# A transformer layer with test-time training: the two MLP weights are read transposed from memory

## The reference, cut to what matters

```python
x = x + layernorm(attn(layernorm(x)))
x = x + layernorm(ffn(layernorm(x)))

def attn(x):                      # 4 heads of 64 for the learned part, 2 of 128 for the attention
    qkv = x @ Wqkv
    q, k, v = heads(silu(qkv))    # q and k divided by their norms
    # scan over 4 chunks of 128 rows, with fast weights W0, W1, W2 and momenta M0, M1, M2 per head
    #   out  = (silu(q W0') * (q W2')) W1'
    #   dW   = gradient of the same form on k, v, times learned rates, plus momentum
    #   W    = renorm(W + newtonschulz5(dW))           # 5 iterations
    ttt = rms_norm(out) * o_norm_g * silu(x @ Ws + bs)
    att = sliding_window_softmax(q_, k_, v_)           # window 128, 2 heads
    return (ttt + att) @ Wo

def ffn(x):
    h = gelu(x @ proj1.T + proj1_bias)                 # proj1 is 1024 x 256
    return h @ proj2.T + proj2_bias                    # proj2 is 256 x 1024
```

## Time and profile before

| | |
|---|---|
| median of 3 runs | 418.66 us (416.7 to 420.85) |
| the profiled execution | 421.38 us, span 419.6 us |
| PE busy | 387.9 us (92%) |
| PE weight loads busy | 311.2 us (74%) |
| DVE busy | 274.4 us (65%) |
| ACT busy | 225.7 us (54%) |
| POOL busy | 195.6 us (47%) |
| mean granted clock of PE | 0.995 of full speed |

### The profile page before, as it was taken

How to read it: one execution, slowest core, us unless ns; L and a number is a source line. 1 busy time by engine, 2 the same in 40 slices (tenths; PEclk the granted TensorE clock), 3 DMA queues, 4 the chain that set the end, 5 groups by cost and what they waited for, 6 DMA issues and landing times.

```text
span 419.6 us, 15701 instructions
## 1 busy us (share of the span) xinstructions
PE 387.9 (92%) x6574; PEld 311.2 (74%) x6574; DVE 274.4 (65%) x720; ACT 225.7 (54%) x444; POOL 195.6 (47%) x273
## 2 busy tenths in 40 slices
PE   5989997999999999999998999988989899997994
PEld 5578766886678869788667888587788647885883
DVE  3468998787265879997446874986667763576013
ACT  1699556466942178646985452654446674433510
POOL 4386671658532524784240874263234260366014
PEclk9999999999999999999999999999999999998999
DMA  5811000000000000030000000001200000020001
GB/s 155 297 39 52 2 2 4 5 4 3 2 4 2 14 2 2 26 118 5 3 2 5 3 2 0 2 2 55 54 5 3 5 1 2 0 74 28 2 0 51
DMA packets 12293, 10.83 MB, mean 26 GB/s; under 512 B 4160, under 2 KB 11712, under 8 KB 12224
## 3 DMA queue, kind: packets, MB, share of 16 engines
q1 hardware_dynamic: 12224, 9.83, 7.5%
HBM read 7.73 MB, written 2.10 MB: 23 GB/s over the span
## 4 chain that ended last, share of the span: by engine, by line
PE 63%; DVE 9%; issue 6%; POOL 5%; DMA 1%; ACT 1%; POOLq 0%; DVEq 0%; SPq 0%; ACTq 0%
PE pair L780 14%; PE pair L789 9%; PE pair L682 6%; PE pair L670 5%; PE pair L695 5%; PE pair L659 4%; PE pair L748 3%; PE pair L564 3%; POOL fro L1386 2%; PE pair L715 2%; PE pair L536 2%; PE pair L621 1%; PE pair L607 1%; POOL u_n L1386 1%; DMA x<-in_L_attn_x_dram 1%
## 5 line engine op out<-in xcount | busy, mean ns | idle before, releaser
L780 PE MATMUL pair<-xn2T,p1T 128*128 128x512 f32 (+1 forms) x160 | 59.8, 524 | 0.6 <-ACT xn2T L813 0.6
L789 PE MATMUL pair<-p2T,h 128*128 128x256 f32 x256 | 56.7, 380 | 0.0
L1391 POOL TENSOR_SCALAR var<-mv 128x1 f32<-128x1 f32 (+1 forms) x52 | 12.4, 238 | 91.8 <-DVE mv L1355 58.8
L789 PEld LDWEIGHTS pair<-p2T,h 128*128 128x128 f32 x256 | 48.2, 190 | 6.5
L780 PEld LDWEIGHTS pair<-xn2T,p1T 128*128 128x128 f32 x160 | 30.5, 197 | 20.0 <-issue 17.5
L1057 DVE SCALAR_TENSOR_TENSOR A<-pair,eye 128x512 f32<-128x512 f32 x45 | 28.6, 684 | 14.3 <-PE pair L670 14.2
L820 ACT ACT_TABLE_LOAD x28 | 35.9, 1283 | 2.1 <-PEq L1532 1.7
L1057 DVE SCALAR_TENSOR_TENSOR B<-pair,eye 128x512 f32<-128x512 f32 x45 | 28.9, 683 | 11.7 <-PE pair L682 11.7
L1033 ACT ACTIVATE h<-pair,b 128x512 f32<-128x512 f32 (+1 forms) x40 | 23.6, 602 | 21.9 <-PE pair L780 21.7
L1386 POOL TENSOR_TENSOR rstd<-var,neg_half 128x1 f32<-128x1 f32 (+1 forms) x52 | 31.7, 610 | 4.3
L682 PE MATMUL pair<-A 64*64 64x64 f32 x1440 | 28.7, 222 | 5.4 <-issue 5.4
(11 more groups left out here) (166 smaller groups left out, 837.2 us busy)
## 6 DMA issues: line engine op xcount, KB each, us to landing
x_in<-in_L_attn_x_dram SPq DMA_DIRECT2D x4, 512.0 KB, 4.3
h<-in_L_ffn_proj_dram SPq DMA_DIRECT2D x2, 1024.0 KB, 6.7
x<-in_L_attn_x_dram SPq DMA_DIRECT2D x4, 512.0 KB, 4.5
out_dram<-rows_a SPq DMA_DIRECT2D x16, 128.0 KB, 1.7
wqkv<-in_L_attn_Wqkv_dram SPq DMA_DIRECT2D x1, 768.0 KB, 5.5
wo<-in_L_attn_Wo_dram SPq DMA_DIRECT2D x1, 256.0 KB, 7.8
X<-in_L_attn_w_dram SPq DMA_DIRECT2D x6, 32.0 KB, 2.4
b<-in_L_ffn_proj_bias_dram SPq DMA_DIRECT2D x1, 128.0 KB, 4.3
```

Source lines behind the costliest of these rows:

```text
L780: mm_ = pe.matmul(ps[:, at], p1T[:, k, n * P:(n + 1) * P], xn2T[:, k, at], start=(k == 0), stop=(k == KC - 1))
L789: mm_ = pe.matmul(ps[:, 0:DIM], h[:, n, b * P:(b + 1) * P], p2T[:, n, :], start=(n == 0), stop=(n == HC - 1))
```

## The change

The host lays proj1 and proj2 out transposed, as 256 x 1024 and 1024 x 256 arrays, before the launch. SP loads them straight into `p1T` and `p2T`. The eight `MT` steps are gone from `ORDER`, from PE and from ACT, with the two views of `h` and the signals `mt_ps` and `mlp_T`. `F1.0.0` and `F2.0.0` wait for the loads instead.

```diff
-    w_sq=1, w_ss=1, w_norm=1, mt_ps=8, mlp_T=8,
+    w_sq=1, w_ss=1, w_norm=1,
...
-    ... TR.0.0 TR.0.1 TR.0.2 MT.0.0
-    LN1.1 KL.0.0 KL.0.1 KL.0.2 KL.0.3 TR.0.3 MT.0.1 MT.0.2 MT.0.3 MT.0.4 MT.0.5 MT.0.6 S.0.0 MT.0.7 S.0.1 TR.0.4
+    ... TR.0.0 TR.0.1 TR.0.2
+    LN1.1 KL.0.0 KL.0.1 KL.0.2 KL.0.3 TR.0.3 S.0.0 S.0.1 TR.0.4
...
-        p1_raw, p2_raw = share(h, 0, HC, DIM), share(h, HC * DIM, KC, HID)
...
-            sp.dma_start(p1_raw[:, :, :], proj1.rearrange("(n p) e -> p n e", p=P)).then_inc(ld_p1, 16)
-            sp.dma_start(p2_raw[:, :, :], proj2.rearrange("(k p) n -> p k n", p=P)).then_inc(ld_p2, 16)
+            sp.dma_start(p1T[:, :, :], proj1T.rearrange("(k p) n -> p k n", p=P)).then_inc(ld_p1, 16)
+            sp.dma_start(p2T[:, :, :], proj2T.rearrange("(n p) e -> p n e", p=P)).then_inc(ld_p2, 16)
...
-            def MT(bank, c, n):
-                ps = take(bank[0], "mlp_T", c, n + 1)
-                pe.wait_ge(ld_p1 if n < 4 else ld_p2, 16)
-                for q in range(4):
-                    ...
-                    mm_ = pe.transpose(ps[:, q * P:(q + 1) * P], blk, ident[:, :])
-                mm_.then_inc(S["mt_ps"].sem, 1)
...
                 if c == 0 and n == 0:
-                    pe.wait_ge(*S["mlp_T"](0, 8))
+                    pe.wait_ge(ld_p1, 16)
...
                 ps = take(bank[0], "f2", c, b + 1)
+                if c == 0 and b == 0:
+                    pe.wait_ge(ld_p2, 16)
...
-                    if c == 0:
-                        act.wait_ge(*S["mt_ps"](0, 8))
...
-            def MT(bank, c, n):
-                act.wait_ge(*S["mt_ps"](c, n + 1))
-                if n < 4:
-                    last = copy(p1T[:, n // 2, (n % 2) * 512:(n % 2 + 1) * 512], BANK[bank[0]])
-                else:
-                    last = copy(p2T[:, 2 * (n - 4):2 * (n - 4) + 2, :].rearrange("p a b -> p (a b)"), BANK[bank[0]])
-                last.then_inc(S["mlp_T"].sem, 1)
...
+_TRANSPOSED = ('L0_ffn_proj1', 'L0_ffn_proj2')
...
-        a = np.ascontiguousarray(inputs[name])
+        a = np.ascontiguousarray(inputs[name].T if name in _TRANSPOSED else inputs[name])
```

More of the change, by code:

```diff
@@ L137 @@
     XT.0 LN1.0 LNX.0 WI.0 VV.0.0 QK.0.0 WN.0 SI.0.0 NQ.0.0 QK.0.1 QK.0.2 SI.0.1 SI.0.2 VV.0.1 VV.0.2 NR.0.0 NQ.0.1
-    NQ.0.2 WX.0.0 WX.0.1 QK.0.3 WX.0.2 SI.0.3 VV.0.3 MS.0 NQ.0.3 SM.0 NR.0.1 NR.0.2 NR.0.3 TR.0.0 TR.0.1 TR.0.2 MT.0.0
-    LN1.1 KL.0.0 KL.0.1 KL.0.2 KL.0.3 TR.0.3 MT.0.1 MT.0.2 MT.0.3 MT.0.4 MT.0.5 MT.0.6 S.0.0 MT.0.7 S.0.1 TR.0.4
+    NQ.0.2 WX.0.0 WX.0.1 QK.0.3 WX.0.2 SI.0.3 VV.0.3 MS.0 NQ.0.3 SM.0 NR.0.1 NR.0.2 NR.0.3 TR.0.0 TR.0.1 TR.0.2
+    LN1.1 KL.0.0 KL.0.1 KL.0.2 KL.0.3 TR.0.3 S.0.0 S.0.1 TR.0.4
     TR.0.5 TR.0.6 TR.0.7 TR.0.8 TR.0.9 SP.0 FW.0.0 FW.0.1 LNX.1 DH.0 FE.0.0 FE.0.1 GB.0.0 GB.0.1 EL.0.0 EL.0.1 ELB.0.0
@@ L187 @@
 SINGLE = {"XT": 2, "MM": 1, "QK": 1, "VV": 1, "TR": 1, "S": 1, "PT": 1, "PV": 1, "CT": 1, "WO": 1, "NT": 1,
-          "F1": 1, "F2": 1, "MT": 1, "SS": 1, "TX": 1, "WX": 1}
+          "F1": 1, "F2": 1, "SS": 1, "TX": 1, "WX": 1}
 PAIRED = ("NA", "NB", "NX", "GB", "FW", "DH", "OUT")
@@ L233, in layer_kernel @@
 def layer_kernel(nc, x, Wqkv, Wlr, Wm, bm, Ws, bs, Wo, w0, w1, w2, o_norm_g, qk_scale, qk_offset,
-                 proj1, proj1_bias, proj2, proj2_bias, out):
+                 proj1T, proj1_bias, proj2T, proj2_bias, out):
     with ExitStack() as ctx:
@@ L756, in NT @@
                 mm_.then_inc(S["nt_ps"].sem, 1)
-            def MT(bank, c, n):
-                ps = take(bank[0], "mlp_T", c, n + 1)
-                pe.wait_ge(ld_p1 if n < 4 else ld_p2, 16)
-                for q in range(4):
-                    if n < 4:
-                        blk = p1_raw[:, 4 * (n % 2) + q, (n // 2) * P:(n // 2 + 1) * P]
-                    else:
-                        col = (2 * (n - 4) + q // 2) * P
-                        blk = p2_raw[:, q % 2, col:col + P]
-                    mm_ = pe.transpose(ps[:, q * P:(q + 1) * P], blk, ident[:, :])
-                mm_.then_inc(S["mt_ps"].sem, 1)
             def F1(bank, c, n, part=None):
@@ L790, in F2 @@
                 mm_.then_inc(S["f2_ps"].sem, 1)
-            parts = {"XT": XT_, "MM": MM, "QK": QK, "VV": VV, "TR": TR, "WX": WX, "MT": MT,
+            parts = {"XT": XT_, "MM": MM, "QK": QK, "VV": VV, "TR": TR, "WX": WX,
                      "GB": GB, "DH": DH, "FW": FW, "OUT": OUT, "DW": DW, "SS": SS, "TX": TX, "NA": NA, "NB": NB, "NX": NX,
@@ L1033, in F1 @@
                 act.activation(h[:, n, at], BANK[bank[0]][:, at], ACT.Gelu, bias=b1[:, n:n + 1]).then_inc(S["h"].sem, 1)
-            parts = {"XT": XT_, "SP": SP, "MS": MS, "QK": QK, "SI": SI, "NQ": SQ, "TR": TR, "WX": WX, "WI": WI, "MT": MT,
+            parts = {"XT": XT_, "SP": SP, "MS": MS, "QK": QK, "SI": SI, "NQ": SQ, "TR": TR, "WX": WX, "WI": WI,
                      "GB": GB, "DH": DH, "FW": FW, "OE": OE, "MU": MU, "TX": TX, "NX": NX, "RN": RN, "S": SC, "PT": PT,
                      "CT": CT, "NT": NT, "F1": F1}
-            WITH_BANK = ("XT", "QK", "TR", "WX", "MT", "TX", "NX", "PT", "CT", "NT", "F1", "GB", "DH", "FW")
+            WITH_BANK = ("XT", "QK", "TR", "WX", "TX", "NX", "PT", "CT", "NT", "F1", "GB", "DH", "FW")
             def run(order):
```

## The result

The changed kernel is a little slower: 422.94 us (median of 20 executions) against 418.37 us, a ratio of 1.0091 with a 95% interval of 1.007 to 1.0112. Weighted by executions the two make 1.007, or 3.0 us, about four times my +0.7 us. On 418.66, the median that I had, this is 421.7, within my range of 415.6 to 422.4 and within the 1% that I had called the same; the first measurement by itself, 422.94, lies 0.5 us above the range.

What follows compares the result with a forecast made beforehand. POOL's qn was taken to release PE at 31.5 us, then DVE to bound the path. Terms 0 + 0 + 0 + 1.5 (clock) - 0.8 (instruction blocks) = +0.7 us on 418.66 gave 419.4 us, range 415.6 to 422.4.

Steps and rivals of the forecast that it cites:

- PE, 32 transposes: PE, 25 to 35 us: removing 4.0 us of transposes gains 0, since POOL's qn until 31.37 covers them.
- ACT, eight copies: ACT, 25 to 35 us: removing 4.4 us of copies gains 0, covered by DVE's run of 10.15 us.
- Loads: Both 1 MB weight loads on SP keep their place; landing later costs nothing, as F1.0.0 starts at 100.42.
- PSUM banks: Bank rotation after the eight MT steps stays; 456 of 458 steps keep their banks, with no wait.
- the waits at 0: PE's waits for the two loads and the dropped wait for ACT's GB.0.0 are met long before: 0.
- The clock: this is the cost I expect: PE, idle mostly from 25.8 to 31.5 us, drops to 1.2 GHz; TR runs slow: +1.5 us, bounds 0.1 to 2.2.
- my 38.7 to 40.8: Expected sign in the profile after: DH on PE ends between 38.7 and 40.8 us, where it was 38.62.
- DVE has no air behind: Behind DH, the dh copies, tanh and EL move with it, and DVE has no idle time to absorb the delay.
- Instruction blocks: -0.8 us: PE's dense 64-wide matmuls: some 70 fewer instructions move the 256-instruction borders, pauses 7.4 to 6.4–6.7 us; bounds -1.7 to +1.7.
- The clock holds: Rival: PE's clock does not fall in the thinned stretch, 25.8 to 31.5 us; 417.9 us, chance 0.23.
- The removed work was on the path: Rival: ACT's copies hold the 25.8 to 31.5 us stage, which gains 2 to 4.4 us; 416.7 to 414.3, chance 0.10.
- The clock stays down: Rival: the slow clock lasts from 31.5 through DH, GB.0.0 and OUT, about 5 us; 423.7 us, chance 0.09.

Runs made afterwards that it cites:

- the kernels with a filling: Kernels with unused work, mostly identity transposes, added in PE's pauses, mostly to the changed kernel; ratios to the kernel before from 0.9922 to 1.0122.
- the padded kernels: Unused 64 x 64 matmuls added on PE: 32 calls to the kernel before, 1.0155; 56 to the changed kernel with 12 transposes, 1.0101.
- the repeat: The changed kernel run again with nothing altered, beside the kernel before: ratio 1.0043, interval 1.0002 to 1.0084.

## Why the prediction was right, and where its size was off

"PE, 32 transposes: taken at 0" and "ACT, eight copies: taken at 0". Right. POOL's qn releases TR.0.4 in both kernels (31.37 and 31.82 us). The kernel with transposes on PE and no copies on ACT is at 0.9999: the copies alone are worth nothing to within 0.4%. The 4.0 us of transposes did cover something, though not by their results: they held the clock, which is the term below.

"Loads", "PSUM banks" and the waits at 0. Right as far as the profile shows: F1.0.0 follows PE's own work without an idle time. No run tested the banks by themselves.

"The clock: this is the cost I expect." The mechanism was right at each link: the fall behind the pause, TR at half its pace, DH late, ACT's and DVE's waits longer. At EL.0.0 the term was 1.5 us taken, 2.2 us as its bound, and 2.46 and 1.15 us measured in the two profiles, so there my figure lay between. The bound was too low for the first profile because I let only the six TR steps run slow; the clock came back at 37.9, and FW (2.34 for 1.98 us) had started slow too. DH's end, 41.37 and 39.96, is outside my 38.7 to 40.8 once and inside once. The pace was right: the 24 transposes took 5.35 us at the lower level, for the 5.38 that I had read off the start. Against this the first profile gave back 0.96 us and the second 0.27, in DVE's elementwise steps around POOL's two products. I had written that DVE has no air behind; it had this.

Over the whole kernel the term was mis-sized: the lower clock costs 3.0 us by the line through the 20, where I had 1.5. F1.0.0 is 1.86 and 2.21 us late, counted from qn. Where the rest lies is open. One candidate is the fall at 301 us in the changed kernel's first profile. It stands behind a border pause of 1.94 us, at a row where the second profile has 1.81 us and no fall behind it, and where the kernel before has 0.41 us; so the change may have made it possible by moving the borders. Two of the kernels with a filling have a fall at 285 and 312 us too, and two profiles can't settle it.

"Instruction blocks: -0.8 us." The sign fits: 4.8 and 6.8 us of pauses in the dense blocks of the changed kernel's two profiles against 8.3 in the earlier trace rows. The size can't be confirmed, since two executions of the same kernel differ by 2 us and both profiles are of executions below their kernel's median. The 3.6 us for each block, on which it rests, did not hold for the padded kernels. That borders matter is shown by them and by the positions of the pauses. My bounds of -1.7 to +1.7 were two pauses either way; they would have been far too narrow for another number of instructions (128 more cost 6.5 us).

So the sum should have read about +3.0 for the clock. With my -0.8 for the borders this makes +2.2, and the 0.8 us to the measured 3.0 is not accounted for.

The rivals. "The clock holds" is excluded as the rule: both profiles have the fall, and the mean clock is 0.984 for 0.993, in none of the first 20 executions above 0.991. One of the 12 of the repeat has 0.993, and at 417.39 us it is also their fastest; there the clock may have held. "The removed work was on the path" is excluded by the kernels with the work put back on one engine each. "The clock stays down": it did for longer than I took, over TR and the start of FW in the first profile, but not through DH, GB and OUT. That its time, 423.7, lies near the measured median does not make its mechanism right.

The Trainium skill ("TensorE: Matmul & The Clock Gate", Part 4) says that transposes do not count as PE being busy in the way that raises the clock. Here 32 transposes of the identity in the pauses took the mean clock from 0.984 to 0.995, and 12 took it to 0.993, so for these float32 transposes the measurement decides against it.

## What to carry to other kernels

Work taken off TensorE inside a stretch where it waits anyway saves nothing, and can cost: if what is left leaves the engine mostly idle, its clock falls and the next steps on the path run at half pace. Look at the granted clock of the stretch behind, and if it falls, try a few cheap transposes in the pause: here 12 of them, on top of the change, gave 0.9964 and 0.9922 against the kernel before, the best kernel of all, some 1.3% under the changed one. When instructions are added or removed ahead of a dense stretch of small matmuls, expect some us from the block borders alone (6.5 and 7.5 us were seen here), and vary the number before judging an idea. Count the instructions in the profile and not in the source: a multiplying call was two loads and two matmuls here, and three of the experiments here did not add the number of instructions that was meant. And read more than one profile: the first two here gave the wrong sign.

## What the runs showed of the hardware that was not expected

The same pause of 2.8 us had the clock fall within it in one profile of the changed kernel, and in the other only in the next pause, 2.9 us later, with the same work of PE ahead; in the three profiles with 12 or 6 transposes ahead of TR.0.4 it fell in neither. A pause of 1.94 us at a border was followed by a fall in one profile, one of 1.81 us in the other was not. So the work that is seen does not by itself say when the clock falls. Why the kernel with 12 transposes is faster than that with 32 (0.9943 as the mean of its two ratios, against 0.9999) is open: its clock is no better (0.9928 against 0.9951), and its pauses in the dense blocks, 7.4 and 4.4 us in two profiles, lie on both sides of the other's 5.8.

Adding 128 instructions of 64 x 64 matmuls to PE in a pause cost 6.5 us, adding 224 cost 7.5 us. PE's pauses in the dense blocks stand at a fixed place in every 256 of its rows in all fourteen profiles.

A product on DVE that starts while POOL works on products of its own ends 0.54 to 0.56 us after POOL's last one, in the three profiles read for it (47.24, 48.31 and 47.58 us, with POOL done at 46.69, 47.75 and 47.04), where such a product takes 0.68 or 0.69 us undisturbed. When the two meet decides how much of the delay was given back, 0.96 us or 0.27.
